# Window attention with smaller value products and split turned probabilities, and a four-way scan whose gated product is formed once, in one four-layer network kernel

## What is computed

```python
q, k, v = split(x @ w_qkv)            # 3 heads of 32
p = softmax(q @ k.T / sqrt(32) + pos_bias)
y = concat_heads(p @ v) @ w_out + b_out
```

```python
a = 1 - sigmoid(delta(x))             # decay
h = scan(a, (1 - a) * B(x) * u(x))    # along rows and columns, forward and backward
y = C(x) * h                          # per direction, then a linear map
m, g = merge(concat_directions(y)) # two linear maps of 256 into 64
out = (m * sigmoid(g)) @ w_o + b_o
```

## Time and profile before

| | us |
|---|---|
| median of three runs | 3772.63 |
| lowest, highest | 3772.1, 3773.64 |
| the profiled execution's own time | 3774.77 |
| its span, first to last instruction | 3773.5 |

### The profile page before, as it was taken

The page is one execution under the profiler, slowest core; times in us unless marked ns, Lnnn a source line. Parts: engine busy times, 40 slices in busy tenths (PEclk is TensorE's granted clock), DMA queues, the critical chain, the costliest instruction groups (busy, mean ns, idle before and its releaser), DMA issues. The chain is left out here.

```text
span 3773.5 us, 70792 instructions
## 1 busy us (share of the span) xinstructions
PE 3208.0 (85%) x21002; PEld 1808.9 (48%) x21002; DVE 2848.4 (75%) x4403; ACT 2471.2 (65%) x4493; POOL 1912.8 (51%) x1754
## 2 busy tenths in 40 slices
PE   5799999989787889999899866887888868788877
PEld 2588888864333444444344322343343324377742
DVE  2566666658526999999999997685999977634467
ACT  4455555558676989889899843684666628744456
POOL 0233333333245889889898865332777753200035
PEclk9899999999898999999999999998999989999999
DMA  4100000002256466575747452220000002230022
GB/s 96 30 14 15 13 15 14 14 24 57 78 152 161 133 192 168 171 193 154 204 137 211 123 141 66 55 56 24 21 21 21 20 22 50 66 77 17 17 53 60
DMA packets 203857, 297.90 MB, mean 79 GB/s; under 512 B 68094, under 2 KB 188210, under 8 KB 203318
## 3 DMA queue, kind: packets, MB, share of 16 engines
q1 hardware_dynamic: 193598, 285.25, 28.6%
q10 hardware_dynamic: 10104, 10.88, 1.2%
HBM read 193.93 MB, written 102.03 MB: 78 GB/s over the span
## 5 line engine op out<-in xcount | busy, mean ns | idle before, releaser
L1761 POOL TENSOR_TENSOR mam_hc<-mam_h,mam_cs 128x896 f32<-128x896 f32 x336 | 703.8, 2095 | 173.3 <-DVE mam_h L1679 85.6
L1679 DVE TENSOR_TENSOR_SCAN mam_h<-mam_a,mam_kept,mam_dbx 128x448 f32<-128x448 f32 x672 | 737.4, 1127 | 33.0 <-ACT mam_a L1553 31.7
L1407 PE MATMUL mam_ps_y<-mam_hc,mam_ident 128*128 128x448 f32 x1344 | 570.5, 558 | 137.3 <-POOL mam_hc L1761 137.1
L1553 ACT ACTIVATE mam_a<-mam_ft,mam_a_neg 128x448 f32<-128x448 f32 x672 | 409.4, 657 | 82.0 <-DVE mam_h L1679 81.2
L1407 PEld LDWEIGHTS mam_ps_y<-mam_hc,mam_ident 128*128 128x128 f32 x1344 | 248.5, 192 | 436.5 <-POOL mam_hc L1761 227.6
L2165 POOL TENSOR_TENSOR scan_ch<-scan_h,scan_cs 128x392 f32<-128x392 f32 x256 | 343.9, 1362 | 197.3 <-DVE scan_h L2109 120.1
L1666 DVE TENSOR_TENSOR mam_dbx<-mam_ps_u,mam_bs 128x448 f32<-128x448 f32 x672 | 380.7, 609 | 23.1 <-DMA mam_bs<-dram_bc 23.1
L792 POOL TENSOR_TENSOR att_prob<-att_prob,att_share 128x588 f32<-128x588 f32 x128 | 151.7, 1185 | 452.7 <-DVE att_share L977 452.7
L366 POOL TENSOR_TENSOR all_x<-all_x,f_yb 128x392 f32<-128x392 f32 x128 | 127.1, 993 | 235.8 <-DVE f_yb L321 235.8
L360 POOL TENSOR_TENSOR all_x<-all_x,f_mixed 128x392 f32<-128x392 f32 x128 | 152.6, 1193 | 184.2 <-DMA f_mixed<-mixed 125.7
L912 ACT ACTIVATE att_pt<-att_ps_t 128x512 f32<-128x512 f32 x128 | 76.4, 597 | 210.2 <-PE att_ps_t L853 210.2
(11 more groups left out here) (249 smaller groups left out, 7713.9 us busy)
## 6 DMA issues: line engine op xcount, KB each, us to landing
mam_taps<-normed SPq DMA_DIRECT2D x220, 130.5 KB
mam_bs<-dram_bc SPq DMA_DIRECT2D x28, 896.0 KB, 14.3
mam_cs<-dram_bc SPq DMA_DIRECT2D x28, 896.0 KB, 16.4
mam_ft<-dram_steps SPq DMA_DIRECT2D x42, 448.0 KB, 4.8
normed<-f_staged SPq DMA_DIRECT2D x384, 38.1 KB
f_mixed<-mixed SPq DMA_DIRECT2D x384, 36.8 KB
dram_gs<-mam_gs SPq DMA_DIRECT2D x56, 224.0 KB, 2.2
mam_gt<-dram_gs SPq DMA_DIRECT2D x48, 224.0 KB, 2.7
```

The lines of the kernel that those rows point to most:

```text
L1407: mm = pe.matmul(ps_y[p % 2][:, 0:MT], ident[:], hc[t % 2][:, i, :], start=False, stop=(t % 8 == 7 and i == 1))
L1553: act.activation(a[t % 3][:, i, :], ft[p % 2][:, 0, :], ACT.Exp, scale=a_neg[:, at:at + 1]).then_inc(decays, 1)
L1679: dve.tensor_tensor_scan(h[:, n % 8, :], a[t % 3][:, i, :], dbx[:, i, 0:MT], kept[:, at:at + 1], ALU.mult, ALU.add).then_inc(scanned, 1)
L1761: pool.tensor_tensor(hc[t % 2][:], h[:, row:row + 2, :], cs[:, 2 * pair:2 * pair + 2, :], ALU.mult).then_inc(weighed, 1)
```

## The change

In attention:

- The rows of a chunk are loaded and windowed twice, at partitions 0 and 96. The values product uses 32 rows: the first half from the copy at 0, the second from the copy at 96. A one-column, one-partition operation on `gate` and waits of GpSimd on itself come with it.
- The turned third head `ps_t2`/`pt2` keeps two pairs of windows on partitions 0 to 63 and two on 64 to 127, so it is half as wide. The lower half is still turned with `pe.transpose`; for the upper half an ordinary product with the identity is used.
- `weigh_values` goes through the windows as i and i + 4: two products on 128 rows, then two on 64 rows (lower, upper), into the two banks of `ps_out`. `finish` takes the banks in two operations.

In the four-scan:

- ScalarE adds the bias to the second image's merge and puts it beside the first image's, in the same bank, so that VectorE forms the gated product in one operation on 128 partitions.
- The product tile of the first direction is held twice (`ch_first`), so GpSimd waits for the merge of the chunk before only ahead of the second direction.
- The stores move from ScalarE's DMA queue to SyncE's, in slot order with the loads; `merge_t` lies in `h[0]`, and the two memsets of `h` go.

The diff, cut to its core:

```diff
+        copies = (0, 96)
+        lower, upper = slice(0, HALF_ROWS), slice(HALF_ROWS, P)
...
-        nvals = buf.sbuf("nvals", [P, 2, 2 * C])
-        rows_in = [buf.sbuf(f"rows_in{p}", [C, ROWS, PAD]) for p in range(2)]
+        nvals = buf.sbuf("nvals", [P, 2 * C])
+        rows_in = [buf.sbuf(f"rows_in{p}", [P, ROWS, PAD]) for p in range(2)]
...
-        pt2 = [buf.sbuf(f"pt2{p}", [P, PAIRS, P]) for p in range(2)]
+        pt2 = [buf.sbuf(f"pt2{p}", [P, PAIRS // 2, P]) for p in range(2)]
...
-        ps_t2 = buf.psum("ps_t2", [P, PAIRS, P])
-        ps_out = buf.psum("ps_out", [P, BANK])
+        ps_t2 = buf.psum("ps_t2", [P, PAIRS // 2, P])
+        ps_out = buf.psum("ps_out", [P, 2, BANK])
...
-                            sp.dma_start(
-                                rows_in[p][:].rearrange("c r q -> c (r q)"),
-                                normed[b, :, bass.ds((t * 2 + p) * NP_ + PAD, NP_)]
-                            ).then_inc(loaded[p], 16)
+                            for at in copies:
+                                sp.dma_start(
+                                    rows_in[p][at:at + C].rearrange("c r q -> c (r q)"),
+                                    normed[b, :, bass.ds((t * 2 + p) * NP_ + PAD, NP_)]
+                                ).then_inc(loaded[p], 16)
...
-                    pool.wait_ge(loaded[p], turn * 16 + 16)
+                    pool.wait_ge(loaded[p], turn * 32 + 32)
...
-                    src = rows_in[p][:, :, 1:SIDE + 1].rearrange("c r (w s) -> c w r s", w=WINS)
-                    dst = xw[p][0:C, :, 0:T].rearrange("c w (r s) -> c w r s", r=WIN)
-                    for half in range(2):
-                        o = pool.tensor_copy(dst[:, 4 * half:4 * half + 4],
-                                             src[:, 4 * half:4 * half + 4])
+                    for at in copies:
+                        if at > 0:
+                            pool.wait_ge(gated, c + 1)
+                            pool.tensor_tensor(gate[0:1, 3:4], gate[0:1, 0:1], gate[0:1, 1:2],
+                                               ALU.add)
+                        src = rows_in[p][at:at + C, :, 1:SIDE + 1].rearrange(
+                            "c r (w s) -> c w r s", w=WINS)
+                        dst = xw[p][at:at + C, :, 0:T].rearrange("c w (r s) -> c w r s", r=WIN)
+                        for half in range(2):
+                            o = pool.tensor_copy(dst[:, 4 * half:4 * half + 4],
+                                                 src[:, 4 * half:4 * half + 4])
                     o.then_inc(windowed, 1)
+                    pool.wait_ge(windowed, c + 1)
...
-                        for half in range(2):
+                        for half, at in enumerate(copies):
                             mm = pe.matmul(ps_vals[64 * half:64 * half + TP,
                                                    win * 2 * C:(win + 1) * 2 * C],
-                                           xw[p][:, win, :], nvals[:, half, :],
+                                           xw[p][at:at + 32, win, :], nvals[at:at + 32, :],
                                            start=True, stop=True)
...
                     for q in range(PAIRS):
                         pe.transpose(ps_t[:, q, :], prob[p][:, 3 * q:3 * q + 2, :].rearrange(
                             "i h j -> i (h j)"), ident[:])
-                        mm = pe.transpose(ps_t2[0:TP, q, :], prob[p][:, 3 * q + 2, :], ident[:])
+                        rows = (lower, upper)[q // 2]
+                        if q < PAIRS // 2:
+                            pe.transpose(ps_t2[rows, q % 2, :], prob[p][:, 3 * q + 2, :], ident[:])
+                        else:
+                            mm = pe.matmul(ps_t2[rows, q % 2, :], prob[p][:, 3 * q + 2, :],
+                                           ident[:], start=True, stop=True)
                     mm.then_inc(turned, 1)
 
                 def weigh_values(c, p):
                     pe.wait_ge(pt_sb, c + 1)
                     pe.wait_ge(pt2_sb, c + 1)
                     reached(pe, resulted, c)
-                    for win in range(WINS):
-                        q, half = win // 2, win % 2
-                        cols = slice(win * T, (win + 1) * T)
-                        pe.matmul(ps_out[0:C, cols], vals[p][:, win, 0:C],
-                                  pt[p][:, q, 64 * half:64 * half + T], start=True, stop=False)
-                        mm = pe.matmul(ps_out[0:C, cols], vals[p][:, win, C:2 * C],
-                                       pt2[p][:, q, 64 * half:64 * half + T], start=False,
-                                       stop=True)
+                    for first in range(WINS // 2):
+                        cols = slice(first * T, first * T + T)
+                        turns = [(bank, first + 4 * bank, (first + 4 * bank) // 2,
+                                  slice(64 * (first % 2), 64 * (first % 2) + T))
+                                 for bank in range(2)]
+                        for bank, win, q, i in turns:
+                            pe.matmul(ps_out[0:C, bank, cols], vals[p][:, win, 0:C],
+                                      pt[p][:, q, i], start=True, stop=False)
+                        for bank, win, q, i in turns:
+                            rows = (lower, upper)[bank]
+                            mm = pe.matmul(ps_out[0:C, bank, cols], vals[p][rows, win, C:2 * C],
+                                           pt2[p][rows, q % 2, i], start=False, stop=True)
                     mm.then_inc(mixed_up, 1)
...
-                    dve.tensor_copy(pt2[p][0:TP], ps_t2[0:TP]).then_inc(pt2_sb, 1)
+                    dve.tensor_copy(pt2[p][:], ps_t2[:]).then_inc(pt2_sb, 1)
...
-                    dve.tensor_scalar(
-                        result[p][:].rearrange("c r (w s) -> c w r s", w=WINS),
-                        ps_out[0:C, 0:N].rearrange("c (w r s) -> c w r s", w=WINS, r=WIN),
-                        b_out[:, 0:1], None, ALU.add).then_inc(resulted, 1)
+                    for bank in range(2):
+                        o = dve.tensor_scalar(
+                            result[p][:].rearrange("c r (w s) -> c w r s", w=WINS)[
+                                :, 4 * bank:4 * bank + 4],
+                            ps_out[0:C, bank, 0:4 * T].rearrange("c (w r s) -> c w r s", w=4,
+                                                                 r=WIN),
+                            b_out[:, 0:1], None, ALU.add)
+                    o.then_inc(resulted, 1)
...
+        product_b = buf.sbuf("product_b", [P, 1])
+        merge_t = h[0][0:LAT].rearrange("m d n -> m (d n)")[:, 0:2 * DIRS * LAT].rearrange(
+            "m (a d o) -> m a d o", a=2, d=DIRS)
+        ch_first = [buf.sbuf(f"ch_first{p}", [P, N]) for p in range(2)]
+        ch = buf.sbuf("ch", [P, DIRS - 1, N])
...
+        def products(n, p):
+            return ch_first[p] if n == 0 else ch[:, n - 1, :]
...
+                def load(f, k):
+
+                    p = k % 2
+                    sp.wait_ge(projected, done(f * K + k - 2, 4))
+                    for image in range(2):
+                        sp.dma_start(
+                            xin[p][32 * image:32 * image + C].rearrange("c r q -> c (r q)"),
+                            normed[f + image * pairs, :, k * NP_ + PAD:k * NP_ + PAD + NP_]
+                        ).then_inc(loaded[p], 16)
+
+                def store(c, p):
+                    sp.wait_ge(resulted, c + 1)
+                    for image in range(2):
+                        sp.dma_start(mixed[c + image * (pairs * K)],
+                                     result[32 * image:32 * image + C]).then_inc(left, 16)
+
+                def slot(f, b, half, k, p, has_tail):
+                    if f is not None and k == 0:
+                        load(f, 0)
+                    if f is not None and k + 1 < K:
+                        load(f, k + 1)
+                    if has_tail:
+                        store(b * K + k - 1, 1 - p)
+
+                stages(sp, slot, store)
...
-                            mm = pe.matmul(ps[:, 0:N], w_merge[rows, n, :], ch[rows, n, :],
+                            mm = pe.matmul(ps[:, 0:N], w_merge[rows, n, :], products(n, p)[rows, :],
...
-                                   bias=merge_b[IMAGE_0, 1:2]).then_inc(sigmoided, 1)
+                                   bias=merge_b[IMAGE_0, 1:2])
+                    act.wait_ge(opened, c + 1)
+                    act.activation(ps_merged[0][IMAGE_1, 0:N], ps_merged[1][IMAGE_1, 0:N],
+                                   ACT.Identity, bias=merge_b[IMAGE_1, 0:1]
+                                   ).then_inc(sigmoided, 1)
...
-                    act.wait_ge(resulted, c + 1)
-                    for image in range(2):
-                        act.dma_start(mixed[c + image * (pairs * K)],
-                                      result[32 * image:32 * image + C]).then_inc(left, 16)
...
-                dve.memset(h[0][:], 0.0)
```

(17 more changed lines are left out.)

38 lines of the change are left out of this document (16 added, 22 removed).

## The result

The changed kernel takes **3931.62 us** (median of 4 runs, 3921.51 to 3939.17), the kernel before 3772.36 us (median of 4, 3771.8 to 3773.64) on the same chip: a ratio of **1.0426**, with a 95% interval of 1.0409 to 1.0443. It is 159 us slower, where 155 was forecast (160 for attention, less 5 for the four-scan). The profiled execution took 3939.17 us, its span 3937.6 us.

What follows compares the result with a forecast made beforehand. TensorE, busy throughout, was taken to bound attention, VectorE (99% busy) the four-scan. Attention +1.25 us a chunk over 128 chunks, +160 us, and four-scan -5 us on 3774.8 gave 3930, as median 3928 us; range 3855 to 3975.

Steps and rivals of the forecast that it cites:

- The price of a switch: TensorE in attention: each change of the array's cut costs 0.11 us in weighing, 0.14 to 0.15 around turning; eleven cost 1.37.
- five holes: TensorE's timeline before: idle gaps of 0.09 to 0.11 us where the cut of the array changes, seen five times.
- A change of rows alone is free: Rival, weighing loop: row changes cost nothing, so weighing saves 0.35 us a chunk; 3828 us in all; chance 0.08.
- Weighing: TensorE, attention: pairing 64-row passes saves 0.35 us, seven changes of cut cost 0.78; sum +0.43 us a chunk.
- turning: TensorE, attention: ordinary products add 0.22 us of streaming, four changes of cut 0.56 to 0.62; sum +0.82 us a chunk.
- values: TensorE, attention: value products on 32 rows instead of 128 save 0, staying at 1.07 us; bounds 0 and 0.24 saved.
- Switches inside a run are free: Rival, attention: switches inside a run of short products cost nothing, -0.13 us a chunk, 3750 us with the scan; chance 0.09.
- values' loads vanish: Rival, attention: the value products' weight loads hide behind passes on other rows, 31 us less, 3897 us; chance 0.06.
- the clock falls: Rival, attention: switches idle the array, clock drops to 1.2 GHz for parts of the stage, +155 us, 4080; chance 0.04.
- GpSimd's second copies hidden by the longer slot: Attention: window copies last some 1.4 us in place of 0.63, ending at about 7, before keys need them at 8.3.
- Four-scan: Four-scan stage: VectorE's product saves 0.63 us, waiting on `rest` leaves 0.09; 0.09 to 0.22 a slot; net -5 us.
- The queue's 3 us: Four-scan: loads behind stores in SP's queue may come late for `decay`, 0.5 us seven times, +3 us.

Runs made afterwards that it cites:

- weigh_grouped: Changed kernel with all 128-row weighing products first, then all 64-row ones: one inner switch in place of seven; 3849.04 us, ratio 1.0208 to the kernel before.
- turn_grouped: Changed kernel with the turning's two ordinary products together at its end, two switches in place of four; 3894.19 us, ratio 1.0325 to the kernel before.
- values_only: Kernel before plus only the second copy of the windows and the value products on 32 rows; 3785.83 us, ratio 1.0038.
- scan_only: Kernel before with only the four-scan part of the change, attention as before; 3772.45 us, ratio 1.0004.

## Why the prediction was right, and where not

- **The price of a switch**: right. 0.11 us was taken for weighing; the trace shows 0.28 and 0.20 us where columns need 0.17 and 0.09, and weigh_grouped 0.67 us for six. 0.14 to 0.15 was taken in the turning; turn_grouped shows 0.29 for two. Of the five holes read as 0.09 to 0.11, the one from values to weighing is 0.12 by its own rows (506.90 to 507.02); it changes nothing.
- **A change of rows alone is free** (rival, 0.08): shown wrong by weigh_grouped. The Trainium skill, "TensorEngine Tiling (Array Packing)", Key Properties, has a change of the tiling mode drain the engine; by that rule, the trace agrees, and it holds for rows alone, at 0.11 us.
- **Weighing** +0.43 forecast, +0.45 measured; **turning** +0.82, and 0.74 + 0.08 = 0.82 measured; **values** 0 and 0; the slot 6.65 and 6.66. 128 slots of +1.26 are 161 us; the stage grew by 166.5. Of the rest (the 127 steps from the first keys product to the last make 160.5), 1.6 lie before the first and 4.4 behind the last one, where the granted clock from 979.8 us on is 0.50 (the 1.2 GHz level; the kernel before keeps 1.00 until its stage ends):

```profile
980.00:988.00 8.00, 6.00 (x42) 3.54 (x42) 1.48 (x4) 0.60 (x1) 0.38 (x1) 0.50 0.02 5
```
- **Switches inside a run are free** (0.09), **values' loads vanish** (0.06), **the clock falls** (0.04): all shown wrong in the same rows, the last by the granted clock of 1.00 in every full slot.
- **GpSimd's second copies hidden by the longer slot**: right. values_only shows what they cost when that cover is gone, 0.2 us in every second chunk, as the text said ("near the path").
- **The sum**: 3928 lies 4 us from the median, closer than its terms. By the stages the change costs 166, not 155 (attention 6.5 us over its term, four-scan 5 over), the profiled executions differ by 164, and the four runs spread over 18 us. The mechanism in attention was right; the last few microseconds of agreement are luck.
- **Four-scan**: the step that failed is "with one product less it would at 2762.72, and waits until about 2763.26. So 0.09 us is left of 0.63". Its times are right (the wait is 0.55 us), but its premise, that VectorE's busy time is the slot, is not: the chain of eight has neither operation in it, and what is left is 0, with or without the copy. The words "by what runs beside them the one on this path may get 0.13 cheaper" had the cause in hand, taken for a small discount when it sets the slot. The forecast of slots of 7.3 to 7.4 us was wrong (7.49); that the term was 5 us and not 30 kept the sum right. The queue's 3 us on the other side were not tested apart, but the trace of scan_only has TensorE waiting on the loads of `scan_xin` 6 times, 5.6 us in all, where before has no such wait. From the first `drive` to the last, the traces with the new stage and its order of work take 445.0 to 446.6 us and those with the old one 444.0 to 445.2 (five each); behind the last `drive`, where only the back part is left, it is 67.6 to 68.7 against 69.8 to 72.1. So there is a loss of about 1 us and a gain of 2 to 3, neither of them where the forecast had it, and the median of scan_only, 1 us slower, can't tell the net from nothing.

## What to carry to other kernels

Count the changes of the array's cut in program order, rows as well as columns, before counting rows saved: with passes of 0.04 us one switch costs 0.11 to 0.15 us, more than two passes, so half-height products pay when they are grouped and lose when they alternate. Where one instruction form shows very different lengths in one stage, put its ends beside the ends on the other engine before believing a busy share: a constant distance from end to end meant here that the two wait for each other inside, and then the order in which they meet was what could be tuned.

## What the runs showed that I had not expected

- Scans on VectorE and products on GpSimd exclude each other, with 0.82 us from one end to the next; taking the gated product off VectorE, outside of that chain, gave nothing.
- A hole in TensorE's stream of 0.13 us behind GpSimd's copies (values_only) shows in no row as a wait for GpSimd, and TensorE counts as 100% busy over it. The starts show it, and the idle time of the weight loads.
